# Layer-1 score and maximum matmuls over 128 zero-padded rows in a two-layer vision transformer

## The chip, the cores and the metric

The kernel runs on one core of a Trainium2 chip. The metric is device time in microseconds (us) of one execution, lower is better.

## What is computed

The input is 16 batches of 1024 tokens with 29 features. The reference embeds them, adds a position table and runs two transformer layers on each batch:

```python
h = tok(x, W)                                   # 1024 x 29 -> 1024 x 128, plus position table
h = h + attn0(layernorm(h))                     # group norm, 8 heads of 64, output projection, residual
h = h + ffn0(layernorm(h))                      # two lower-triangular 128 x 128 maps, gelu between
h = h + attn1(layernorm(h))                     # 8 heads of 16
h = h + switch_ffn(layernorm(h))                # 16 experts, one per token, capacity limit
# in both attentions, for every head of every batch:
scores = Q @ K.T * scale                        # 1024 x 1024
out = softmax(scores) @ V
```

The first layer (layer 0 below) has heads of 64 columns, the second (layer 1) heads of 16.

## The kernel before

Each head's softmax needs the row maxima before the exponentials. So the kernel computes all scores twice. The *maximum* pass (`max_tile`, TensorE at L766) makes 16 tiles of 128 queries by 512 keys for each head; VectorE reduces each to its row maximum (L1466). The maxima are transposed (L772), negated and copied to SBUF (L1022), and a DMA writes them as one more row of the query operand. The *score* pass (`scores`, TensorE at L790 and L792) makes tiles of 128 keys by 512 queries that already hold score minus maximum; ScalarE takes the exponential of each into `pr` (L1038).

For accuracy with matmuls in the fp32r format, every operand is split into a high and a low part, and the parts are stacked along the contraction rows. These operands are the *stacks*. In layer 0 a head's stacks fill 128 rows, with a second operand of 65 rows for the low terms and the maximum. In layer 1 a head has 16 columns, so a stack is 3 x 16 = 48 rows of products and row 48 for the maximum (a row of ones on the key side, minus the maximum on the query side). Before the change, one tile `stacks1[128, 2, 1024]` holds two heads of layer 1 at once: an even head in partitions 0 to 63, an odd head in partitions 64 to 127. The layer-1 maximum matmul contracts over 48 rows and its score matmul over 49. The stacks are filled by SP's DMA queue (`stack1` calls `move` with five copies; the fifth writes the row of ones), and `row` writes the maxima.

The exponentials times the values are `values0` (L808 for the high half, L809 for the low half, bf16, 129 columns each; the low half `pr_lo` is made at L461 by VectorE or GpSimd) and `values1` (L821, layer 1, four matmuls side by side on 32 output columns each, then `fold1` at L830). `outputs0` on VectorE (L1495, L1496) adds the high and low value sums of layer 0 into `on`, `normalize0` on GpSimd (L1183) scales them in place, and `heads_turn` on TensorE transposes 128 columns of `on` (two heads, a *chunk* c) for the output projection.

All engines follow one order written out in tables. A *unit* is 512 queries of one head, eight *steps* of 128 keys. There are five kinds of segment: "first" (layer 0 of batch 0, 16 units), "second" (layer 0 of batch 1 with layer 1 of batch 0, 32 units), "loop" (13 turns of 32 units; it also routes and runs the experts of the batch before, L752 and L1456), "penult" (as loop) and "final" (layer 1 of the last batch, 16 units). In the three kinds with both layers the units alternate: a layer-0 unit, then a layer-1 unit. Beside the score matmuls of a unit run the maximum tiles that `tile_step` gives (in a layer-1 unit, tiles of layer 1: in one layer-1 unit of two those of the same head, in the other those of the next head) and, at four of the eight steps (`VALUE_STEPS`), a fourth of the values of the unit before: sixteen L808 and L809 matmuls in a layer-1 unit, L821 and L830 in a layer-0 unit. After the units of a segment comes a serial part (`serial`): projections, norms, the feed-forward part.

A step of TensorE's order is:

```python
for step, at, layer, u, kt in steps_of(seg.kind):
    scores(seg, at, layer, u, kt)
    for tile in due_tiles(seg.kind, step):
        max_tile(seg, "now", *tile)
    if at > 0 and kt in VALUE_STEPS:
        values(seg, at - 1, VALUE_STEPS.index(kt))
```

The score pass and the maximum pass have two PSUM banks each, so TensorE waits when ScalarE has not taken the exponential two tiles back, or VectorE not the maximum two tiles back. VectorE works through one list in order: low parts, maxima, outputs, then experts.

Of the kernel before, what the change touches and what calls it, by code (L numbers as in the profile page):

```python
# [8 lines left out]
F32 = mybir.dt.float32  # L9
F32R = mybir.dt.float32r  # L10
# [5 lines left out]
P = 128  # L16
# [10 lines left out]
def units_of(kind):  # L27

    if kind == "first":
        return [(0, u) for u in range(16)]  # L30
    if kind == "final":
        return [(1, u) for u in range(16)]
    return [(layer, u) for u in range(16) for layer in range(2)]
# [245 lines left out]
def build(nc, x, tok_w, gn_w, gn_b, wq, bq, wk, bk, wv, bv, wo, bo, w1, b1, w2, b2,  # L279
          wq1, wk1, wv1, bq1, bk1, bv1, wo1, bo1, sw, sb_, ew, eb, pe, tri, out):  # L280
    NB, HH, WW, FT = x.shape
    S = HH * WW
    T = S // P
    C = tok_w.shape[1]
    H0, D0 = 8, 64
    H1, D1 = wq1.shape[0], wq1.shape[2]
    E = sw.shape[0]
    CAP = float(int(1.2 * (NB * S) / E))
    INNER = H0 * D0
# [4 lines left out]
    with ExitStack() as ctx:  # L294
        def sb(name, shape, dt=F32):
            return ctx.enter_context(nc.sbuf_tensor(name, shape, dt))

        def sem(name):
            return ctx.enter_context(nc.semaphore(name))
# [5 lines left out]
        ones = sb("ones", [P, P])  # L305
# [45 lines left out]
        k_lo, k_hi, q_hi, q_lo = (parts[:, n, :] for n in range(4))  # L351
        stacks = sb("stacks", [P, 2, 4, S], F32R)
        kB, kA, qA, qB = (stacks[:, :, n, :] for n in range(4))
        stacks1 = sb("stacks1", [P, 2, S], F32R)
        pr = sb("pr", [P, 2, T, HALF])
        pr_lo = sb("pr_lo", [P, T, HALF], BF16)
        mxh = sb("mxh", [P, 2, T, 2])
# [2 lines left out]
        o_hi = sb("o_hi", [P, 2, 2, D0])  # L360
        o_r = sb("o_r", [P, 4, 2])
        o_r1 = sb("o_r1", [P, 2, 4])
        on = sb("on", [P, T, INNER])
        on1 = sb("on1", [P, T, P])
        lg = sb("lg", [P, T, E])
        ex = sb("ex", [P, T, E])
# [18 lines left out]
        prep_pe = sem("prep_pe")  # L385
        prep_dve = sem("prep_dve")
        prep_pool = sem("prep_pool")
        x_loaded = Counts(sem("x_loaded"), 16)
        out_stored = Counts(sem("out_stored"), 16)
        hm_copied = Counts(sem("hm_copied"), 1)  # L390
# [39 lines left out]
        def await_drained(eng, seg, *names):  # L430
            plan = PLANS[seg.kind][0]
            for b in range(2):
                uses = [plan[name][1] for name in names if plan[name][0] == b]
                if uses:
                    eng.wait_ge(glue_drained[b].sem, glue_drained[b].at(seg, max(uses) + 1))
# [30 lines left out]
                    yield 8 * at + kt, at, layer, u, kt  # L466

        def k_stack(layer, head):
            return kB[:, head % 2] if layer == 0 else stacks1[64 * (head % 2):64 * (head % 2) + 64, 0, :]

        def q_stack(layer, head):
            return qB[:, head % 2] if layer == 0 else stacks1[64 * (head % 2):64 * (head % 2) + 64, 1, :]

        def max_row(layer):
            return 64 if layer == 0 else 3 * D1
# [4 lines left out]
        def await_stack(eng, b, layer, head):  # L480
            signal = stack_in(layer, head)
            eng.wait_ge(signal.sem, signal.at(b, 16 * (3, 5)[layer] * (head // 2 + 1)))

        @block.sync
        def _(sp):
# [23 lines left out]
                    sp.dma_start(dst, src).then_inc(load_small, 16)  # L509
            slot_free = sp.alloc_register("slot_free")  # L510
            sp.wait_ge(prep_dve, PREP_DVE)

            def load_x(b):
                sp.dma_start(xin[:, :, :], x_v[b.index()]).then_inc(x_loaded.sem, 16)

            def move(layer, head, moves):
                for dst, src in moves:
                    sp.dma_start(dst.bitcast(F32), src.bitcast(F32)).then_inc(stack_in(layer, head).sem, 16)
# [8 lines left out]
            def stack1(head, src):  # L527
                a, b_ = D1 * head, D1 * head + D1
                kk, qq = k_stack(1, head), q_stack(1, head)
                move(1, head, [(kk[0:2 * D1], src[a:b_, 0:2, :]),  # L530
                               (qq[0:2 * D1], src[a:b_, 2:3, :].broadcast_to([D1, 2, S])),
                               (kk[2 * D1:3 * D1], src[a:b_, 1, :]), (qq[2 * D1:3 * D1], src[a:b_, 3, :]),
                               (kk[3 * D1:3 * D1 + 1].rearrange("a (t q) -> a t q", t=T), ones[0:T, :])])

            def row(seg, name, layer, head, g):
                n = 2 * layer + g
# [66 lines left out]
        def _(te):  # L603
# [19 lines left out]
            def use(seg, name, *after):  # L623

                plan = PLANS[seg.kind][0]
                b, k = plan[name]
                needs = {b: k}
                for bank, count in (plan[other] for other in after):
                    needs[bank] = max(needs.get(bank, 0), count + 1)
                for bank, count in needs.items():  # L630
                    te.wait_ge(glue_drained[bank].sem, glue_drained[bank].at(seg, count))
                return glue[b], glue_filled[b].sem

            def turn(seg, name, src, rows_=P):
                bank, filled = use(seg, name)
                for j in range(4):
                    last = te.transpose(bank[0:rows_, j * P:(j + 1) * P], src(j), ident)
                last.then_inc(filled, 1)
# [45 lines left out]

            def heads_turn(seg, c, g):
                te.wait_ge(on_ready.sem, on_ready.at(seg.l0, 8 * (c + 1)))
                turn(seg, f"oT0.{c}.{g}", lambda j: on[:, 4 * g + j, c * P:(c + 1) * P])

            def done_heads(seg):
                AT = turn_slots(seg.kind)  # L690
# [64 lines left out]
            def max_tile(seg, when, layer, head, n):  # L755
                b = seg.layer(layer) if when == "now" else seg.following(layer)
                k = TILE_PLACES[seg.kind][when, layer, head, n]
                t, g = n // 2, n % 2
                if n == 0:
                    await_stack(te, b, layer, head)  # L760
                te.wait_ge(max_reduced.sem, max_reduced.at(seg, k - 1))
                if layer == 0:
                    qs, ks = qA[:, head % 2], kA[:, head % 2]
                else:
                    qs, ks = q_stack(1, head)[0:3 * D1], k_stack(1, head)[0:3 * D1]
                mm(maxb[k % 2][:, :], qs[:, t * P:(t + 1) * P], ks[:, g * HALF:(g + 1) * HALF],  # L766
                   start=True, stop=True).then_inc(max_filled.sem, 1)

# [13 lines left out]
            def scores(seg, at, layer, u, kt):  # L782
                b, k, head, g = seg.layer(layer), 8 * at + kt, u // 2, u % 2
                if kt == 0:
                    arrived = mrow_in[2 * layer + g]
                    te.wait_ge(arrived.sem, arrived.at(b, 16 * (head + 1)))
                te.wait_ge(exp_done.sem, exp_done.at(seg, k - 1))
                bank, q, kk = score[k % 2], slice(g * HALF, (g + 1) * HALF), slice(kt * P, (kt + 1) * P)
                if layer == 0:
                    mm(bank[:, :], kA[:, head % 2, kk], qA[:, head % 2, q], start=True, stop=False)  # L790
                last = max_row(layer) + 1
                mm(bank[:, :], k_stack(layer, head)[0:last, kk], q_stack(layer, head)[0:last, q],  # L792
                   start=(layer == 1), stop=True).then_inc(score_filled.sem, 1)

# [344 lines left out]
        def _(pool):  # L1139
# [38 lines left out]
            def normalize0(seg, at, jj):  # L1178
                _, u = units_of(seg.kind)[at]
                head, n, t = u // 2, 2 * u + jj, 4 * (u % 2) + 2 * jj  # L1180
                pool.wait_ge(o_drained.sem, o_drained.at(seg, o_place(seg.kind, 0, u, jj) + 1))
                o = on[:, t:t + 2, head * D0:(head + 1) * D0]
                pool.tensor_tensor(o, o, o_r[:, n % 4, :].unsqueeze(2).broadcast_to([P, 2, D0]), ALU.mult)\  # L1183
                    .then_inc(on_ready.sem, 1)

# [72 lines left out]
        def _(dve):  # L1258
            dve.memset(ones[:, :], 1.0).then_inc(prep_dve, 1)
            dve.memset(kB[64:65, :, :].bitcast(F32), 1.0)  # L1260
            dve.memset(v0[:, :, :, 2 * D0:2 * D0 + 2], 1.0)
            dve.memset(v1[:, :, :], 0.0).then_inc(prep_dve, 1)
            dve.memset(seen[:, :], 0.0)
# [4 lines left out]
            for n in range(2):  # L1268
                last = dve.tensor_tensor(pr[:, 1, 0, n * P:(n + 1) * P], pr[:, 0, 0, n * P:(n + 1) * P], lower, ALU.mult)
            last.then_inc(prep_dve, 1)  # L1270
            dve.wait_ge(prep_dve, 3)
            for c in range(NCH):
                last = dve.tensor_scalar(pr[:, 1, 1, c * P:(c + 1) * P], ones[:, :], bv_c[:, c:c + 1], None, ALU.mult)
# [213 lines left out]
            def outputs0(seg, at, jj):  # L1487
                _, u = units_of(seg.kind)[at]
                n, own = o_place(seg.kind, 0, u, jj), 2 * u + jj
                head, t = u // 2, 4 * (u % 2) + 2 * jj  # L1490
                dve.wait_ge(o_hi_out.sem, o_hi_out.at(seg, n + 1))
                bank = obank[n % 2][:, :].rearrange("p (j n) -> p j n", j=2)
                if own >= 4:
                    dve.wait_ge(on_ready.sem, on_ready.at(seg.l0, own - 3))
                dve.reciprocal(o_r[:, own % 4, :], bank[:, :, 2 * D0])  # L1495
                dve.tensor_tensor(on[:, t:t + 2, head * D0:(head + 1) * D0], bank[:, :, D0:2 * D0],  # L1496
                                  o_hi[:, own % 2, :, 0:D0], ALU.add).then_inc(o_drained.sem, 1)

            def outputs1(seg, at):
# [165 lines left out]
```

## Time and profile before

| | |
|---|---|
| three runs | median 9110.86 us (9104.55 to 9149.21) |
| profiled execution, its own time | 9088.71 us |
| its span, first to last instruction | 9086.9 us |
| TensorE busy in the span | 7605.5 us (84%) |
| VectorE / ScalarE / GpSimd busy | 57% / 36% / 18% |
| mean granted TensorE clock | 0.791 of full speed |

The profile is one execution. A busy TensorE is not necessarily one at its peak: matmuls are pipelined, and the granted clock has two levels, 1.0 (2.4 GHz) and 0.5 (1.2 GHz). A stretch with clock c spent 2 x (1 - c) of its time at the lower level. Durations of single matmuls overlap with their neighbours', so the cost of one is read from the distance between starts.

### The profile page before, as it was taken

How to read it: one execution, taken by the hardware profiler on the slowest of the kernel's cores; microseconds unless marked ns; L12 is line 12 of the kernel's file. 1: busy time of each engine (PE TensorE's matmuls, PEld its weight loads, DVE VectorE, ACT ScalarE, POOL GpSimd, SP SyncE). 2: the span in 40 equal slices, each digit the busy share in tenths (PEclk: the TensorE clock that was granted, in tenths of full speed). 3: DMA queues.
4: the chain of work that ended last, by engine and by line, in shares of the span. 5: the costliest groups of instructions: out<-in, count | busy, mean ns of one | idle time of the engine just before them, and what ended most of it. 6: DMA issues, size and time to landing. Idle time of an engine off the chain costs nothing.

```text
span 9086.9 us, 124508 instructions
## 1 busy us (share of the span) xinstructions
PE 7605.5 (84%) x39399; PEld 4583.5 (50%) x39399; DVE 5140.1 (57%) x11577; ACT 3263.9 (36%) x6291; POOL 1680.7 (18%) x1623
## 2 busy tenths in 40 slices
PE   6798888878888788887888878888787887879886
PEld 4565554445545455454554545555454554545542
DVE  5565656556555565655656555565565555655554
ACT  3343433334333343333433334333343333433331
POOL 2222211111111121111111111121111111111110
PEclk8887877878778787787877878777787777877877
DMA  2221101111021110211102111021111111101100
GB/s 58 51 44 28 36 21 46 36 31 36 21 46 35 31 40 16 54 27 37 36 14 54 27 39 36 12 54 27 39 36 23 44 27 39 36 22 43 27 23 9
DMA packets 89196, 309.01 MB, mean 34 GB/s; under 512 B 23942, under 2 KB 30022, under 8 KB 78278
## 3 DMA queue, kind: packets, MB, share of 16 engines
q1 hardware_dynamic: 88518, 300.53, 14.6%
q8 instruction: 357, 5.85, 0.3%
q14 instruction: 321, 2.63, 0.1%
HBM read 49.33 MB, written 41.94 MB: 10 GB/s over the span
## 4 chain that ended last, share of the span: by engine, by line
issue 67%; POOL 14%; PE 13%; DVE 4%; DMA 1%; POOLq 0%; SPq 0%; ACT 0%; DVEq 0%; ACTq 0%
POOL pr_lo L461 9%; PE bank L792 2%; POOL on L1183 2%; PE bank L766 2%; POOL on L1191 2%; PE bank L808 1%; PE bank L752 1%; PE bank L809 1%; PE bank L821 1%; PE bank L790 1%; DVE hm L1456 1%; DVE mxh L1466 1%; DMA stacks<-parts 1%; POOL rs L1158 1%; DVE pr_lo L461 0%
## 5 line engine op out<-in xcount | busy, mean ns | idle before, releaser
L1466 DVE TENSOR_REDUCE mxh<-bank 128x1 f32<-128x512 f32 x4096 | 2770.7, 688 | 2843.3 <-PE bank L766 2822.6
L1038 ACT ACTIVATE pr<-bank 128x512 f32<-128x512 f32 x4096 | 2410.2, 598 | 3065.4 <-PE bank L792 2984.8
L766 PE MATMUL bank<-stacks 128*128 128x512 f32 (+1 forms) x4096 | 2048.6, 509 | 860.9 <-DVE mxh L1466 824.8
L792 PE MATMUL bank<-stacks 65*128 65x512 f32 (+1 forms) x4096 | 2027.9, 502 | 11.8 <-ACT pr L1038 9.5
L766 PEld LDWEIGHTS bank<-stacks 128*128 128x128 f32 (+1 forms) x4096 | 910.4, 226 | 1265.3 <-DVE mxh L1466 1094.7
L808 PE MATMUL bank<-v,pr 128*128 128x129 bf16 x8192 | 1470.2, 269 | 3.3 <-DVE mT L461 2.4
L809 PE MATMUL bank<-v,pr_lo 128*128 128x129 bf16 x7936 | 1436.4, 270 | 0.0
L461 POOL TENSOR_TENSOR pr_lo<-pr 128x1024 bf16<-128x1024 f32 x496 | 938.8, 1893 | 2254.0 <-ACT pr L1038 2252.3
L792 PEld LDWEIGHTS bank<-stacks 65*128 65x128 f32 (+1 forms) x4096 | 875.0, 217 | 820.1 <-issue 573.6
L808 PEld LDWEIGHTS bank<-v,pr 128*128 128x128 bf16 x8192 | 988.5, 123 | 450.9 <-issue 444.6
L790 PE MATMUL bank<-stacks 128*128 128x512 f32 x2048 | 1111.0, 542 | 49.7 <-issue 41.7
L809 PEld LDWEIGHTS bank<-v,pr_lo 128*128 128x128 bf16 x7936 | 978.9, 123 | 0.0
L1183 POOL TENSOR_TENSOR on<-on,o_r 128x128 f32<-128x128 f32 x512 | 217.1, 424 | 3708.2 <-DVE on L1496 3708.2
L790 PEld LDWEIGHTS bank<-stacks 128*128 128x128 f32 x2048 | 424.4, 207 | 559.9 <-issue 423.8
L752 PE MATMUL bank<-ewT,mT 128*128 128x512 f32 x1024 | 652.6, 727 | 44.6 <-DVE hm L1456 44.6
L821 PE MATMUL bank<-pr,v 128*32 128x512 f32 x4096 | 650.7, 766 | 12.0 <-ACT pr L1038 12.0
L461 DVE TENSOR_TENSOR pr_lo<-pr 128x1024 bf16<-128x1024 f32 x496 | 603.5, 1217 | 40.1 <-ACT pr L1038 40.1
L1022 ACT ACTIVATE mrow<-bank 4x128 fp32r<-4x128 f32 x512 | 135.1, 264 | 1323.9 <-PE bank L772 1321.5
L1456 DVE SCALAR_TENSOR_TENSOR hm<-bank,wgt,hm 128x128 f32<-128x128 f32 x2048 | 552.4, 343 | 55.7 <-PE bank L752 48.6
L821 PEld LDWEIGHTS bank<-pr,v 128*32 128x32 f32 x4096 | 127.9, 130 | 360.5 <-issue 351.1
L1191 POOL TENSOR_TENSOR on<-on,o_r 128x64 f32<-128x64 f32 x256 | 192.1, 750 | 626.3 <-DVE on L1508 626.3
L973 ACT ACTIVATE parts<-bank,cols 128x512 fp32r<-128x512 f32 x256 | 176.2, 688 | 333.9 <-PE bank L648 330.2
(180 smaller groups left out, 5709.1 us busy)
## 6 DMA issues: line engine op xcount, KB each, us to landing
stacks<-parts SPq DMA_DIRECT2D x384, 512.0 KB, 6.7
parts_d<-pr SPq DMA_DIRECT2D x16, 2048.0 KB, 7.1
stacks<-parts_d SPq DMA_DIRECT2D x224, 128.0 KB
stacks<-parts_d SPq DMA_DIRECT2D x224, 64.0 KB
stacks<-mrow SPq DMA_DIRECT2D x512, 2.0 KB
out<-hm SPq DMA_DIRECT2D x16, 512.0 KB, 2.7
stacks<-pr SPq DMA_DIRECT2D x32, 128.0 KB
stacks<-pr SPq DMA_DIRECT2D x32, 64.0 KB
```

The lines of the kernel that those rows point to most:

```text
L461: return eng.tensor_tensor(low_of(seg.kind, u, kt - 1).rearrange("p a b -> p (a b)"), w, hi, ALU.subtract)
L752: mm(bank[:, :], mT[:, t * P:(t + 1) * P], ewT[:, 4 * q:4 * q + 4, :].rearrange("p e f -> p (e f)"), start=True, stop=True).then_inc(fille ...
L766: mm(maxb[k % 2][:, :], qs[:, t * P:(t + 1) * P], ks[:, g * HALF:(g + 1) * HALF], start=True, stop=True).then_inc(max_filled.sem, 1)
L790: mm(bank[:, :], kA[:, head % 2, kk], qA[:, head % 2, q], start=True, stop=False)
L792: mm(bank[:, :], k_stack(layer, head)[0:last, kk], q_stack(layer, head)[0:last, q], start=(layer == 1), stop=True).then_inc(score_filled.s ...
L808: mm(dst, hi, v0[:, kt, head, 0:w], start=(kt == 0), stop=False)
L809: last = mm(dst, lo, v0[:, kt, head, 0:w], start=False, stop=(kt == T - 1))
L821: last = mm(obank[n % 2][QUAD * r:QUAD * (r + 1), :], v1[:, kt, col:col + QUAD], pr[:, at % 2, kt, :], start=(kt < 4), stop=(kt >= 4))
L1038: act.activation(pr[:, at % 2, kt, :], score[k % 2][:, :], ACT.Exp, scale=SCALES[layer]).then_inc(exp_done.sem, 1)
L1183: pool.tensor_tensor(o, o, o_r[:, n % 4, :].unsqueeze(2).broadcast_to([P, 2, D0]), ALU.mult)\
L1456: ins = dve.scalar_tensor_tensor(hm[:, t, :], bank[:, e * P:(e + 1) * P], wgt[:, t, 4 * q + e:4 * q + e + 1], hm[:, t, :], ALU.mult, ALU.add)
L1466: dve.tensor_reduce(mxh[:, layer, n // 2, n % 2:n % 2 + 1], maxb[k % 2][:, :], AX_X, ALU.max)\
```

## The change

`stacks1` gets one tile of 128 rows for each of the two head buffers and each operand: `[128, 2, 2, 1024]`. It is filled with zeros once, in VectorE's prologue, and both head parities now lie in partitions 0 to 48. The layer-1 maximum and score matmuls contract over all 128 rows. The maximum matmul now also covers row 48, so the fifth copy of `stack1`, which wrote ones into the key side, instead writes a row of zeros (row 127 of the query side) over the old maxima of the query side; the ones are written once by two DMAs in SP's prologue, with a wait of their own (`ones_in`). `on` shrinks from four chunks of 128 columns to two that are used in turn, and `outputs0` waits at units 8 and 12 until the transposes of the chunk it overwrites have been drained.

```diff
-        stacks1 = sb("stacks1", [P, 2, S], F32R)
+        stacks1 = sb("stacks1", [P, 2, 2, S], F32R)
-        on = sb("on", [P, T, INNER])
+        on = sb("on", [P, T, 2 * P])
+        ones_in = sem("ones_in")
         def k_stack(layer, head):
-            return kB[:, head % 2] if layer == 0 else stacks1[64 * (head % 2):64 * (head % 2) + 64, 0, :]
+            return kB[:, head % 2] if layer == 0 else stacks1[:, head % 2, 0, :]
         def q_stack(layer, head):
-            return qB[:, head % 2] if layer == 0 else stacks1[64 * (head % 2):64 * (head % 2) + 64, 1, :]
+            return qB[:, head % 2] if layer == 0 else stacks1[:, head % 2, 1, :]
             sp.wait_ge(prep_dve, PREP_DVE)
+            for n in range(2):
+                sp.dma_start(stacks1[3 * D1:3 * D1 + 1, n, 0, :].rearrange("a (t q) -> a t q", t=T).bitcast(F32), ones[0:T, :])\
+                    .then_inc(ones_in, 16)
+            sp.wait_ge(ones_in, 32)
                                (kk[2 * D1:3 * D1], src[a:b_, 1, :]), (qq[2 * D1:3 * D1], src[a:b_, 3, :]),
-                               (kk[3 * D1:3 * D1 + 1].rearrange("a (t q) -> a t q", t=T), ones[0:T, :])])
+                               (qq[3 * D1:3 * D1 + 1], qq[P - 1:P])])
-                turn(seg, f"oT0.{c}.{g}", lambda j: on[:, 4 * g + j, c * P:(c + 1) * P])
+                turn(seg, f"oT0.{c}.{g}", lambda j: on[:, 4 * g + j, c % 2 * P:(c % 2 + 1) * P])
-                    qs, ks = q_stack(1, head)[0:3 * D1], k_stack(1, head)[0:3 * D1]
+                    qs, ks = q_stack(1, head), k_stack(1, head)
-                last = max_row(layer) + 1
+                last = max_row(0) + 1 if layer == 0 else P
-                o = on[:, t:t + 2, head * D0:(head + 1) * D0]
+                o = on[:, t:t + 2, head % 4 * D0:(head % 4 + 1) * D0]
             dve.memset(kB[64:65, :, :].bitcast(F32), 1.0)
+            dve.memset(stacks1[:, :, :, :].bitcast(F32), 0.0)
+                if u in (8, 12) and jj == 0:
+
+                    await_drained(dve, seg, f"oT0.{u // 4 - 2}.0", f"oT0.{u // 4 - 2}.1")
-                dve.tensor_tensor(on[:, t:t + 2, head * D0:(head + 1) * D0], bank[:, :, D0:2 * D0],
+                dve.tensor_tensor(on[:, t:t + 2, head % 4 * D0:(head % 4 + 1) * D0], bank[:, :, D0:2 * D0],
```

## Rows read from the trace of the kernel before

**Rows 1.** The page: TensorE's share of the span, and its clock in 40 slices (tenths).
```profile
PE 7605.5 (84%) x39399; PEld 4583.5 (50%) x39399; DVE 5140.1 (57%) x11577; ACT 3263.9 (36%) x6291; POOL 1680.7 (18%) x1623
...
PEclk8887877878778787787877878777787777877877
```

**Rows 2.** Groups by shape: count | busy us, mean ns of one | idle before.
```profile
L792 PE MATMUL bank<-stacks 49*128 49x512 f32 x2048 | 1147.8, 574 | 11.8 <-ACT pr L1038 9.5 <-DMA stacks<-mrow 0.2
L766 PE MATMUL bank<-stacks 48*128 48x512 f32 x2048 | 1127.3, 563 | 537.0 <-DVE mxh L1466 527.0 <-DMA stacks<-ones 5.1
...
L792 PE MATMUL bank<-stacks 65*128 65x512 f32 x2048 | 880.1, 430 | 0.0
```

**Rows 3.** Attention of whole segments (loop turns 1 and 5, second, final): stretch, length, busy, PEclk.
```profile
861.30:1344.70 483.40, 428.13 (x2251) 261.77 (x2249) 271.71 (x590) 181.93 (x356) 88.06 (x87) 0.78 0.12 27
...
3137.00:3604.30 467.30, 411.13 (x2251) 252.44 (x2249) 270.68 (x588) 181.50 (x356) 88.04 (x87) 0.81 0.12 28
...
8741.70:8963.30 221.60, 190.37 (x736) 76.63 (x734) 127.82 (x343) 83.19 (x162) 7.50 (x24) 0.75 0.05 15
...
402.40:773.30 370.90, 353.82 (x2135) 227.37 (x2133) 222.56 (x410) 177.51 (x352) 91.06 (x78) 0.82 0.15 33
```

**Rows 4.** Layer-0 units of loop turn 6: one unit, and the sum over its 16.
```profile
3858.90:3873.00 14.10, 12.14 (x53) 6.19 (x51) 8.87 (x20) 5.34 (x12) 4.18 (x3) 0.88 0.11 30
...
sum 200.80, PE 179.88 PEld 104.52 DVE 133.46 ACT 88.87 POOL 66.48; mean PE 11.24 PEld 6.53 DVE 8.34 ACT 5.55 POOL 4.16
```

**Rows 5.** Layer-1 units of the same turn: two of the 16, and their sum.
```profile
3821.70:3834.90 13.20, 12.81 (x96) 7.75 (x95) 9.10 (x17) 7.40 (x16) 1.97 (x3) 1.00 0.01 1
...
3873.00:3895.60 22.60, 19.01 (x88) 11.60 (x88) 9.50 (x23) 5.55 (x11) 0.69 (x2) 0.62 0.00 0
...
sum 267.20, PE 232.82 PEld 148.66 DVE 137.24 ACT 92.61 POOL 21.60; mean PE 14.55 PEld 9.29 DVE 8.58 ACT 5.79 POOL 1.35
```

**Rows 6.** A stretch inside the second of these units.
```profile
3881.00:3894.60 13.60, 13.60 (x62) 8.14 (x61) 2.94 (x6) 2.82 (x6) 0.40 (x1) 0.50 0.00 0
```

**Rows 7.** Timeline where that unit begins: start, length, engine, line [idle before].
```profile
3874.38 2.16 DVE L1456 SCALAR_TENSOR_TENSOR hm<-bank,wgt,hm 128x128 f32<-128x128 f32 x8
...
3876.45 1.22 DVE L461 TENSOR_TENSOR pr_lo<-pr 128x1024 bf16<-128x1024 f32 x1
...
3878.32 0.79 PE L766 MATMUL bank<-stacks 48*128 48x512 f32 x1 [3.59 <-DVE mxh L1466]
```

**Rows 8.** TensorE's timeline in a layer-1 unit, same head in both passes, clock 1.0.
```profile
3831.24 0.22 PE L809 MATMUL bank<-v,pr_lo 128*128 128x129 bf16 x1
3831.39 0.50 PE L792 MATMUL bank<-stacks 49*128 49x512 f32 x1
3831.73 0.39 PE L766 MATMUL bank<-stacks 48*128 48x512 f32 x1
3832.05 0.23 PE L808 MATMUL bank<-v,pr 128*128 128x129 bf16 x1
```

**Rows 9.** The same in the first segment, where all operands have over 64 rows.
```profile
102.59 0.40 PE L792 MATMUL bank<-stacks 65*128 65x512 f32 x1
102.83 0.40 PE L766 MATMUL bank<-stacks 128*128 128x512 f32 x1
103.07 0.23 PE L808 MATMUL bank<-v,pr 128*128 128x129 bf16 x1
```

**Rows 10.** TensorE's timeline in a layer-1 unit whose maximum tiles are the next head's.
```profile
3802.65 0.49 PE L792 MATMUL bank<-stacks 49*128 49x512 f32 x1
3802.65 0.49 PE L766 MATMUL bank<-stacks 48*128 48x512 f32 x1
3802.98 0.39 PE L792 MATMUL bank<-stacks 49*128 49x512 f32 x1
3802.99 0.39 PE L766 MATMUL bank<-stacks 48*128 48x512 f32 x1
```

**Rows 11.** Timeline of the prologue: VectorE's fill of v1 and its next wait.
```profile
3.70 1.06 DVE L1262 MEMSET v<- 128x1208 f32 x1 [0.20 <-issue]
...
20.61 0.37 DVE L1267 TENSOR_REDUCE fold<-tri_sb 128x32 f32<-128x128 f32 x1 [15.61 <-DMA pr<-in_L_ffn_switch_b]
```

**Rows 12.** The page, DMA issues: KB each, us from issue to landing.
```profile
xin<-in_x SPq DMA_DIRECT2D x16, 116.0 KB, 2.0
```

## The prediction

> **What bounds the kernel now.** I read the page first. TensorE is busy for 84% of the span, VectorE for 57%, and TensorE's clock stands at seven or eight tenths in nearly every slice, never at ten [rows 1]. So the busiest engine also runs slowly for a good part of the time.
>
> The second view is the groups by shape. A layer-1 score matmul (49 rows) takes 574 ns on average, a layer-0 one with the same 512 columns 430 ns [rows 2]. Where the clock is 1.0, both take 0.40 to 0.50 us [rows 8, 9]. So what differs is not the price of a row, but the clock under which each kind happens to run.
>
> The third view asks what the clock is worth. Two loop turns do the same work, 2251 matmuls each: one takes 483.4 us at 0.78, the other 467.3 us at 0.81 [rows 3]. The first spent 0.44 x 483.4 = 213 us at the lower level, the second 0.38 x 467.3 = 178 us. So 35 us more at the lower level cost 16.1 us: 0.46 us for each. It would be 0.5 if TensorE alone set the time. I use 0.45 (all turns that I compared lie near it). The kernel is bound by TensorE, and by TensorE's clock.
>
> The fourth view says where the low time lies. I cut one loop turn into its 32 units. Adding 2 x (1 - clock) x length over them, the 16 layer-0 units spent 43 us of 200.8 us at the lower level [rows 4], the 16 layer-1 units 138 us of 267.2 us [rows 5]. The reader is to compare two neighbours. The layer-0 unit at 3858.9 has the clock 0.88 over 14.1 us, so 3.4 us low: it falls and is back at once [rows 4]. The layer-1 unit behind it has 0.62 over 22.6 us, so 17.2 us low [rows 5]. It begins with 3.59 us in which TensorE waits: VectorE works through eight expert updates (2.16 us) and a low part (1.22 us) before it takes the next maximum [rows 7]. The clock falls there and then doesn't come back, though TensorE is busy without a gap: for 13.60 of 13.60 us at 0.50 [rows 6]. What sets it apart from a layer-0 unit is the rows: of a layer-1 unit's columns about half (sixteen matmuls of 512 against 64 of 129) pass over 48 or 49 rows. A layer-1 unit can also keep the full clock (3821.7, 1.00, 13.2 us [rows 5]); it has a head's projections with 128 rows in it.
>
> So the trace speaks for a clock that follows how many rows of the array work, not only for how long it is busy. The Trainium skill, "TensorE: Matmul & The Clock Gate", Part 1, says that the clock is set by how busy TensorE has been recently and rises after sustained activity; the stretch of 13.60 us fully busy at 0.50 doesn't agree with that if busy means any matmul.
>
> **The change part by part.**
>
> *Layer-1 matmuls over 128 rows, effect on the clock.* Nothing about a matmul's own columns changes. The layer-1 stretches get the shapes of the layer-0 stretches. The falls themselves stay, since their cause is VectorE's list. What should change is the recovery. In a loop turn 13 of the 16 layer-1 units have low time, 3.4 us at the least and 17.4 us at the most, 138 us in all; two of them stand in [rows 5]. If each of the 13 recovers as the layer-0 unit does, in 3.4 us, 44 us are left. If each needs twice that, 88 us. If the padding also stops the falls, 0. I take 50 us, near the first, because that is the nearest row. The saving is 88 us low, times 0.45 = 40 us a turn. The 13 turns and "penult" make 14: 554 us. Bounds: 14 x 0.45 x 50 = 315 us and 14 x 0.45 x 138 = 870 us.
>
> "Second" takes 370.9 us at 0.82, so 133 us low, and "final" 221.6 us at 0.75, so 111 us low [rows 3]. "Second" has no experts, and "final" only a few beside layer 1. I take 80 us off each, times 0.45 = 36 us each, 72 us. Bounds 40 and 100 us. The serial parts and "first" have none of these matmuls and keep their time.
>
> *Effect on the order of matmuls, same head.* In half of the layer-1 units both passes work on one head. With values around them the distances between starts at full clock are 0.15 (L809 to L792), 0.34 (L792 to L766) and 0.32 us (L766 to L808): 0.81 us [rows 8]. Where all operands exceed 64 rows, the second and third are 0.24 and 0.24 us [rows 9], and from one value matmul to the next it is 0.06 us, the nearest row for the first. That is 0.54, or 0.27 us less, at four steps a unit. There are 15 segments with 8 such units: 120 x 4 x 0.27 = 130 us. The Trainium skill, "TensorEngine Tiling (Array Packing)", Key Properties, says that changing the tiling mode drains TensorE; the extra 0.08 to 0.10 us on both sides of the value matmuls is what such a drain would show as, and by it these gaps go.
>
> *Next head.* In the other half the score matmul and the maximum matmul lie in different halves of the partitions, and they start at the same 0.01 us: pairs every 0.33 us, both for the price of one [rows 10]. Padded, they need 0.24 each. At the four steps with values the old chain is 0.15 + 0 + 0.42 = 0.57 us (the 0.42 is the pair's 0.33 and the extra 0.09) against 0.54; at the four others 0.33 against 0.48. That is 4 x 0.15 less 4 x 0.03 = 0.48 us worse: 120 x 0.48 = 58 us lost. At the lower level all of these distances about double. The Trainium skill, "TensorE: Matmul & The Clock Gate", in its closing table, speaks against this change: small-K matmuls in distinct row groups run concurrently, and K = 32 alone takes as long as K = 128; the trace agrees with the pairs, and padding gives this up.
>
> Both together: 130 - 58 = 72 us, times 0.9 for what lies on the path (0.45 of 0.5): 65 us. Bounds: 130 us gained, if the lost pairs are hidden behind ScalarE; and if the extra gaps stay, nothing is gained and eight pairs a unit cost 0.24 us each, 120 x 8 x 0.24 x 0.9 = 207 us lost.
>
> *Zeros and ones.* VectorE fills 4096 columns; 1208 took 1.06 us, so 3.6 us, ahead of a wait of 15.61 us for loads [rows 11]: nothing, and 3.6 us without that cover. SP issues two small DMAs and waits for them before the first `load_x`. The nearest row is 2.0 us to landing [rows 12], plus two issues: 3 us, once, on the path, between 0 and 5. Behind that wait stand SP's first load and all of the embedding.
>
> *The fifth copy of `stack1`.* A row of 4 KB from one partition replaces eight pieces of 512 B, at the same place in SP's queue. TensorE waited 5.1 us in all on the old one [rows 2], so the effect is between a gain of 5 us and a few us lost: nothing. The stacks are due 24 steps before their first tile, so a faster TensorE doesn't overtake them.
>
> *`on` in two chunks.* Units 8 and 12 wait for the drain of transposes that were issued at steps 78 and 142, while the outputs come at steps 140 and 204 (in "first" at 44 and 76 against 76 and 108). With 32 steps and more between them the wait has been met when it is reached, so it costs nothing. Were it not, VectorE's maxima would queue behind it, and TensorE behind these.
>
> *Sum.* 554 + 72 + 65 - 3 = 688 us less. From the profiled execution's 9088.7 us (span 9086.9) that is 8401 us. The median shown lies 0.24% higher, so 8420 us. I say 8410.
>
> **The rivals.**
>
> *A: likeliest.* As summed. With all bounds at one end it is 9111 - 870 - 100 - 130 = 8011 us, with all at the other 9111 - 315 - 40 + 207 + 5 = 8968 us. They won't all fall on one side; its own range is 8150 to 8700 us. Chance 0.68.
>
> *B: the clock rises, VectorE takes the time.* At full clock TensorE's idle gaps behind VectorE weigh more, each can bring a new fall, and layer-1 units with experts stay near 18 us instead of 22.6. For it: L766 already waited 527 us for VectorE [rows 2], and the stall of 3.59 us has nothing to do with TensorE [rows 7]. Against it: a unit with 9.10 us of VectorE's work was done in 13.2 us at full clock [rows 5]. About half of the gain remains: 8750 us (8700 to 8900). Chance 0.13.
>
> *C: the clock doesn't follow the padded rows.* The clock may look only at busy time, or rows of zeros may not count as work. No matmul of this trace multiplies stacks of zeros, so no row excludes it. Against the first, the 13.60 us at 0.50 [rows 6]. Then the order's 65 us remain, and 3 us are lost: 9050 us, between 8980 and 9110. By the Trainium skill's rule of the busy TensorE ("TensorE: Matmul & The Clock Gate", Part 1) this case, with its 9050 us, is the one to expect. Chance 0.12.
>
> *D: slower.* C, and the drains stay as well, so that only the lost pairs are left. 120 units x 8 pairs make 960. Each costs 0.24 us at full clock and twice that, 0.48, at the lower level, 0.36 in the middle: 346 us, times 0.9 = 311 us, so 9422 us. It decides as soon as the clock in layer-1 units stays under about 0.80 and the gaps of [rows 8] don't shrink; the pairs of [rows 10] speak for it. Chance 0.07.
>
> **How the numbers follow.** 0.5% of 9111 us is 46 us, about what a measurement of this kernel can tell from no change. A and B are faster. C is faster by over 46 us in 0.07 and within it in 0.05. D is slower. That makes 0.88, 0.05 and 0.07. A and B hold 0.81, so the range is theirs: 8150 to 8900.
>
> **What would show it.** The mean clock of the span rises from 0.79 to about 0.86; that of layer-1 units to near 0.88, with no stretch of over 10 us at 0.50 in them. L766 and L792 of layer 1 come to 430 to 470 ns mean, all start apart, and the distances of [rows 8] become those of [rows 9]. Serial parts keep their length. If the clock stays at 0.79, C or D is right, and the distances tell which. If it rises and units with experts don't shrink below 18 us, it is B. The forecast is wrong in size if the falls themselves vanish (faster than 8150) or recovery takes longer than a layer-0 unit's.

## The result, and the profile after

The changed kernel takes 8245.07 us in the median (8236.99 to 8252.57, 4 runs) against 9107.70 us of the kernel before (9100.57 to 9149.21, 4 runs). The ratio is 0.9044, with a 95% interval of 0.9015 to 0.9074. The profiled execution took 8252.57 us, its span is 8250.8 us, its mean granted clock 0.861. The forecast of 8410 us (8150 to 8900) lies on the right side, and the time lies inside its range; the gain is 863 us where 700 were forecast.

The page, TensorE's and the clock's lines, answer to [rows 1]:

```profile
PE 6712.0 (81%) x39399; PEld 4321.9 (52%) x39399; DVE 5134.2 (62%) x11578; ACT 3222.9 (39%) x6291; POOL 1681.3 (20%) x1623
...
PEclk8898888889888898888988889888898888989887
```

The number of matmuls is the same. No slice of the clock is below 8 but the last. The groups by shape (count | busy us, mean ns of one | idle before) answer to [rows 2]:

```profile
L771 PE MATMUL bank<-stacks 128*128 128x512 f32 x4096 | 1858.3, 456 | 937.5 <-DVE mxh L1472 900.0 <-DMA stacks<-parts 23.4 <-DMA stacks<-stacks 5.1
...
L797 PE MATMUL bank<-stacks 128*128 128x512 f32 x2048 | 1095.1, 537 | 8.0 <-ACT pr L1043 7.9
...
L797 PE MATMUL bank<-stacks 65*128 65x512 f32 x2048 | 862.1, 421 | 0.0
```

The new fifth copy (`stacks<-stacks`) holds TensorE up for 5.1 us in all, as the old one did.

The attention of a loop turn, of "second" and of "final" (stretch, length, busy times, PEclk), answer to [rows 3]:

```profile
1321.00:1741.20 420.20, 360.00 (x2251) 238.26 (x2249) 271.08 (x588) 178.81 (x357) 88.09 (x87) 0.89 0.14 31
404.40:718.80 314.40, 293.94 (x2135) 202.61 (x2133) 222.02 (x410) 175.06 (x352) 91.10 (x78) 0.97 0.18 39
7925.60:8126.20 200.60, 168.52 (x736) 88.58 (x735) 127.08 (x343) 84.13 (x162) 7.48 (x23) 0.88 0.06 17
```

A turn's attention took 467.3 and 483.4 us in [rows 3]; the one shown here takes 420.2 us. "Second" went from 370.9 to 314.4 us, "final" from 221.6 to 200.6 us. The same turn as in [rows 4] and [rows 5] cut into its units: first a layer-0 unit and the sum over the 16 of layer 0, then two layer-1 units and the sum over their 16.

```profile
4022.30:4036.40 14.10, 11.95 (x53) 6.71 (x52) 9.05 (x20) 5.26 (x12) 4.19 (x3) 0.88 0.10 30
...
sum 201.30, PE 179.17 PEld 106.41 DVE 136.09 ACT 88.74 POOL 65.56; mean PE 11.20 PEld 6.65 DVE 8.51 ACT 5.55 POOL 4.10
```

```profile
3987.90:3999.60 11.70, 10.72 (x96) 7.94 (x95) 8.97 (x17) 6.99 (x14) 2.04 (x3) 1.00 0.01 2
...
4036.40:4052.70 16.30, 12.62 (x87) 9.09 (x86) 9.33 (x23) 5.21 (x11) 0.69 (x2) 0.79 0.00 0
...
sum 218.60, PE 180.65 PEld 131.84 DVE 134.84 ACT 90.07 POOL 22.54; mean PE 11.29 PEld 8.24 DVE 8.43 ACT 5.63 POOL 1.41
```

All of this turn's gain lies in the layer-1 units: 267.2 us became 218.6 us. The unit of 22.6 us at 0.62 [rows 5] takes 16.3 us at 0.79, 6.8 us of it low instead of 17.2. Added up over the 16 units, 50 us are low instead of 138. Also look at the first of the two. It had the full clock before as well, and still went from 13.2 to 11.7 us. So the clock isn't all.

### The profile page after: what moved, and what is told of

The parts are those of the page before. It is cut to its first block, busy times and chain, and to the rows that moved or that the text cites. A ratio compares the mean times of both kernels' runs of the same rounds, so it can differ in the third digit from the quotient of the medians.

```text
span 8250.8 us, 124569 instructions
## 1 busy us (share of the span) xinstructions
PE 6712.0 (81%) x39399; PEld 4321.9 (52%) x39399; DVE 5134.2 (62%) x11578; ACT 3222.9 (39%) x6291; POOL 1681.3 (20%) x1623
## 4 chain that ended last, share of the span: by engine, by line
issue 65%; POOL 16%; PE 12%; DVE 4%; DMA 1%; POOLq 1%; SPq 0%; ACT 0%; DVEq 0%; ACTq 0%
POOL pr_lo L462 9%; PE bank L771 2%; POOL on L1188 2%; POOL on L1196 2%; PE bank L797 2%; PE bank L757 1%; DVE mxh L1472 1%; PE bank L813 1%; DVE hm L1462 1%; PE bank L814 1%; PE bank L826 1%; PE bank L795 1%; DMA stacks<-parts 1%; POOL rs L1163 1%; DVE pr_lo L462 1%
## 5 line engine op out<-in xcount | busy, mean ns | idle before, releaser
L771 PE MATMUL bank<-stacks 128*128 128x512 f32 x4096 | 1858.3, 456 | 937.5 <-DVE mxh L1472 900.0
L797 PE MATMUL bank<-stacks 65*128 65x512 f32 (+1 forms) x4096 | 1957.3, 479 | 8.0 <-ACT pr L1043 7.9
L771 PEld LDWEIGHTS bank<-stacks 128*128 128x128 f32 x4096 | 850.5, 208 | 1452.3 <-DVE mxh L1472 1193.2
L813 PE MATMUL bank<-v,pr 128*128 128x129 bf16 x8192 | 1229.5, 242 | 3.3 <-DVE mT L462 2.4
L814 PE MATMUL bank<-v,pr_lo 128*128 128x129 bf16 x7936 | 1176.0, 240 | 0.0
L795 PE MATMUL bank<-stacks 128*128 128x512 f32 x2048 | 1073.9, 524 | 47.2 <-issue 40.9
L813 PEld LDWEIGHTS bank<-v,pr 128*128 128x128 bf16 x8192 | 871.6, 109 | 296.1 <-issue 277.3
L797 PEld LDWEIGHTS bank<-stacks 65*128 65x128 f32 (+1 forms) x4096 | 837.8, 205 | 320.1 <-issue 178.1
L814 PEld LDWEIGHTS bank<-v,pr_lo 128*128 128x128 bf16 x7936 | 865.6, 109 | 0.0
L795 PEld LDWEIGHTS bank<-stacks 128*128 128x128 f32 x2048 | 410.9, 201 | 508.7 <-issue 347.9
L826 PE MATMUL bank<-pr,v 128*32 128x512 f32 x4096 | 617.4, 730 | 12.0 <-ACT pr L1043 12.0
L757 PE MATMUL bank<-ewT,mT 128*128 128x512 f32 x1024 | 568.7, 641 | 42.9 <-DVE hm L1462 42.9
```

Of the source, the lines that this page charges most:

```text
L757: mm(bank[:, :], mT[:, t * P:(t + 1) * P], ewT[:, 4 * q:4 * q + 4, :].rearrange("p e f -> p (e f)"), start=True, stop=True).then_inc(fille ...
L813: mm(dst, hi, v0[:, kt, head, 0:w], start=(kt == 0), stop=False)
L814: last = mm(dst, lo, v0[:, kt, head, 0:w], start=False, stop=(kt == T - 1))
L826: last = mm(obank[n % 2][QUAD * r:QUAD * (r + 1), :], v1[:, kt, col:col + QUAD], pr[:, at % 2, kt, :], start=(kt < 4), stop=(kt >= 4))
```

## The experiments

Two theories stood against each other at first. **R**: the clock follows the rows of the array in use. **M**: what counts is to stay in shapes of over 64 rows; the gaps at each alternation go, and the clock rises because of that. Each pad size is an edit of two lines of the changed kernel; N is 48 and 49, 64, 65 or 96:

```diff
-                    qs, ks = q_stack(1, head), k_stack(1, head)
+                    qs, ks = q_stack(1, head)[0:N], k_stack(1, head)[0:N]
-                last = max_row(0) + 1 if layer == 0 else P
+                last = max_row(0) + 1 if layer == 0 else N
```

**48 and 49 rows.**

> The changed kernel, but the layer-1 matmuls contract over 48 and 49 rows of the padded tiles again, both heads in partitions 0 to 48. No pairs can form. Theory R (the clock follows the rows of the array in use): the mean clock falls back to 0.77 to 0.80 and the time lies above the kernel before, 9150 to 9450 us, since the pairs are gone and the extra gaps beside the value matmuls stay. Theory B (the gain came from something other than rows, such as one tile per head, the ones written once or the two chunks): the time stays near 8250 us.

Measured: 9516.3 us, ratio 1.045 (1.0378 to 1.0523), span 9512.1 us, clock 0.761. Its page:

```profile
PEclk8877777777777777777777777777787777877766
```

The clock lies just below R's range and the time above it, on R's side and far from B's. The whole gain hangs on the rows; of ones written once, one tile per head and two chunks no gain is left to see. The kernel is 425 us of span slower than the one before, since the pairs are gone as well. But most of that is the clock again: 4547 us are low instead of 3798, which at 0.45 makes 337 us, and 88 us are left for the pairs as such.

**65 rows.**

> The changed kernel with 65 rows in both layer-1 matmuls. More than 64 rows, so the extra gaps of 0.08 to 0.15 us beside the value matmuls should be gone as with 128 rows, but little over half of the rows are in use. Theory R: the clock is between, 0.80 to 0.84, and the time 8600 to 8950 us. Theory M (what counts is to stay in the mode of over 64 rows, and the clock rose only because the gaps went): clock 0.86 and 8250 to 8300 us.

Measured: 8605.84 us, ratio 0.945 (0.9374 to 0.9527), span 8588.5 us, clock 0.821. R, at the lower end of the time. M as it stands falls: in shapes of over 64 rows throughout, the clock is still far from 0.861.

**96 rows.**

> The changed kernel with 96 rows. Theory R: most of the gain, clock 0.84 to 0.86, 8280 to 8500 us, between 65 and 128 rows. Theory M: the same as 65 and 128 rows, 8250 to 8300 us.

Measured: 8363.55 us, ratio 0.9184 (0.9117 to 0.9252), span 8370.1 us, clock 0.846. With 65, 96 and 128 rows the clock is 0.821, 0.846 and 0.861 and the span 8588.5, 8370.1 and 8250.8 us: more rows of zeros, a faster kernel. In low time (2 x (1 - clock) x span) these are 3075, 2578 and 2294 us. So 781 us less of it saved 338 us, 0.43 us each; the forecast used 0.45. None of these three kernels crosses 64 rows in layer 1, and their columns are the same, so this line shows the effect of the rows by itself.

**Halves of 64 rows.** The kernel before, with each half of its one tile padded to 64 rows. The pairs of [rows 10] stay possible. The ones are again written once by two DMAs in SP's prologue; those lines are left out here:

```diff
+            dve.memset(stacks1[:, :, :].bitcast(F32), 0.0)
-                               (kk[3 * D1:3 * D1 + 1].rearrange("a (t q) -> a t q", t=T), ones[0:T, :])])
+                               (qq[3 * D1:3 * D1 + 1], qq[63:64])])
-                    qs, ks = q_stack(1, head)[0:3 * D1], k_stack(1, head)[0:3 * D1]
+                    qs, ks = q_stack(1, head), k_stack(1, head)
-                last = max_row(layer) + 1
+                last = max_row(0) + 1 if layer == 0 else 64
```

> The kernel before with its two heads in the halves of one tile, but each padded with zeros to 64 rows, so that the matmuls use 64 rows and the next head's maxima can still run at the same time as the scores. Theory R: a little of the clock comes back (48 and 49 rows become 64), mean 0.80 to 0.83 and 8750 to 9050 us. Theory M: nothing changes against before, 9080 to 9130 us, since the gaps stay.

Measured: 8857.43 us, ratio 0.9727 (0.9653 to 0.98), span 8866.9 us, clock 0.811. R again: here the shapes alternate exactly as often as before (2794 changes between at most 64 rows and over 64 in both traces), and the clock still rises.

**64 rows, the next size below 65.**

> The changed kernel with 64 rows in both layer-1 matmuls, against the run with 65: one row less, but the shapes alternate again between at most 64 and over 64 rows, 2726 times in the program. Theory G (each of these alternations costs a gap of about 0.1 us beside the clock): 200 to 320 us above the 65-row run, 8800 to 8930 us, with the clock down by no more than 0.01 or 0.02. Rival (gaps are hidden, all of the difference is low time): within 60 us of the 65-row run. Against the kernel with halves of 64 rows, which has the pairs: 100 to 300 us slower if the pairs are worth what the run with 49 rows suggests.

Measured: 9083.85 us, ratio 0.9986 (0.9969 to 1.0004), span 9110.6 us, clock 0.802. One row less costs 478 us, more than theory G said, and the rival's 60 us is excluded. (The two ran on different chips; by their ratios to the kernel before, 0.9986 and 0.945, it comes out the same.) Its low time is 3608 us, 533 more than with 65 rows, which at 0.45 explains 240 us of the 522 us between the spans. The other 282 us go to the alternations. The traces have 2794 changes between at most 64 rows and over 64 with 64 rows, and 100 with 65; the expectation's 2726 also counts changes to matmuls of at most 32 rows. So it is 0.10 us for each of 2694. A layer-1 unit at full clock in both shows them without the clock. First with 64 rows, then with 65:

```profile
4409.40:4422.60 13.20, 12.79 (x95) 7.77 (x95) 9.07 (x17) 7.42 (x16) 2.04 (x3) 1.00 0.00 1
```

```profile
4155.30:4167.10 11.80, 10.83 (x96) 8.02 (x95) 8.98 (x17) 7.08 (x15) 2.09 (x3) 1.00 0.01 2
```

The same unit at the same clock takes 1.4 us less. The waits of TensorE's weight loads for "issue" (in total, times, longest), again 64 rows and then 65:

```profile
PEld bank L797 <- issue: 614.4, 1276, 1.7
PEld bank L813 <- issue: 477.3, 1013, 0.7
```

```profile
PEld bank L813 <- issue: 313.8, 947, 0.5
PEld bank L797 <- issue: 186.6, 679, 1.7
```

The gap can also be read without any price for the clock. I took each entry into a group of layer-1 matmuls together with the exit behind it, wherever both traces have the same clock and TensorE isn't idle, and compared the distances between the same starts. With 64 rows an entry and its exit take 0.31 us more at clock 1.0 (463 places) and 0.36 us more at 0.5 (204 places). For the 1347 entries that would be some 410 to 490 us of TensorE's own time (an estimate); 282 us of it reached the time of the kernel.

The Trainium skill, "TensorEngine Tiling (Array Packing)", Key Properties, says that a change of the tiling mode drains TensorE. These runs agree that such a change costs time: the step from 64 to 65 rows removes about 0.10 us of the kernel's time an alternation.

Against the halves of 64 rows the run is 244 us longer in span, with 256 us more low time (115 us). About 129 us are left for the pairs that the halves can run at once.

**The two chunks of `on` alone**, on the kernel before.

> The kernel before with only the two chunks of on and the wait at units 8 and 12. Both theories: no change, 9050 to 9150 us (ratio 0.998 to 1.002), since the transposes waited for were drained 32 steps and more earlier.

Measured: 9151.6 us against 9122.65 us, ratio 1.0024 (1.0005 to 1.0042). No gain; if anything it costs 0.2%, at the edge of what was expected (ratio up to 1.002).

**The changed kernel again, and nonzero rows.** The second kernel fills the pad rows of the key side with 0.7:

```diff
-            dve.memset(stacks1[:, :, :, :].bitcast(F32), 0.0)
+            dve.memset(stacks1[:, :, 0, :].bitcast(F32), 0.7)
+            dve.memset(stacks1[:, :, 1, :].bitcast(F32), 0.0)
```

> The changed kernel once more, on the same chip as the next two, 8230 to 8260 us, to compare them with it.

> The changed kernel with the key side's pad rows filled with 0.7 instead of zeros; the query side's pad rows stay zero, so the products don't change. Theory R: rows count as rows whatever is in them, ratio to the changed kernel 0.998 to 1.002. Theory Z (zeros count for less): the clock rises further, by 0.005 or more, and the time falls below 8220 us.

Measured: 8243.59 us (ratio to before 0.9029, 0.9005 to 0.9053) and 8248.29 us (0.9033, 0.9009 to 0.9058), clocks 0.863 and 0.862. Rows of zeros on the key side count like any. With both sides nonzero nothing was tried, since the sums would change.

**Layer 0 padded too.** Its second score operand has 65 rows. Rows 64 to 127 of `kB` and `qB` are filled with zeros once, and the matmul uses 128 (the line that makes `zeroed` is left out):

```diff
+            for n in range(2):
+                dve.memset(kB[64:128, n, :].bitcast(F32), 0.0)
+                dve.memset(qB[64:128, n, :].bitcast(F32), 0.0).then_inc(zeroed, 1)
+            dve.wait_ge(zeroed, 2)
             dve.memset(kB[64:65, :, :].bitcast(F32), 1.0)
-                last = max_row(0) + 1 if layer == 0 else P
+                last = P
```

> The changed kernel, and also the second operand of the layer-0 score matmul padded from 65 to 128 rows with zeros. Theory R: the layer-0 units lose some of their low time too (their clock is 0.90 on average, 40 us low of 201 us a turn), mean clock 0.87 to 0.88, 8130 to 8220 us. Theory M (only the mode of over 64 rows counts): no change, since 65 rows are already in that mode.

Measured: 8129.98 us, ratio to before 0.8906 (0.8883 to 0.893), clock 0.877. That is 114 us below the changed kernel on the same chip. Here no shape newly crosses 64 rows, and no column is added. M expected no change, R forecast it.

**Short updates.** What is left of the low time? The start of the unit at 4036.4 answers to [rows 7]:

```profile
4037.85 2.16 DVE L1462 SCALAR_TENSOR_TENSOR hm<-bank,wgt,hm 128x128 f32<-128x128 f32 x8
...
4039.93 1.22 DVE L462 TENSOR_TENSOR pr_lo<-pr 128x1024 bf16<-128x1024 f32 x1
...
4041.80 0.79 PE L771 MATMUL bank<-stacks 128*128 128x512 f32 x1 [3.68 <-DVE mxh L1472]
```

The wait is as long as before, and the L771 behind it takes 0.79 us again.

```diff
-dve.scalar_tensor_tensor(hm[:, t, :], bank[:, e * P:(e + 1) * P], wgt[...], hm[:, t, :], ...)
+dve.scalar_tensor_tensor(hm[:, t, 0:8], bank[:, e * P:e * P + 8], wgt[...], hm[:, t, 0:8], ...)
```

> The changed kernel with the expert updates of VectorE cut from 128 to 8 columns (the other 120 columns of the expert sum are left out), so that the eight updates take about 0.6 us instead of 2.16. Theory S (what is left of the low time in layer-1 units begins in VectorE's list, when TensorE waits for the maxima): the low time of the units with experts falls, mean clock 0.87 to 0.90, 7900 to 8100 us. Rival (the falls have another cause): only the stall itself shrinks, the clock stays at 0.86 to 0.865, 8100 to 8180 us.

Measured: 7726.19 us, ratio 0.85 (0.8424 to 0.8576), span 7753.2 us, clock 0.894. The kernel leaves out 120 of the 128 columns of the expert sum, so it only measures. Theory S holds; the time is below its range of 7900 to 8100 us, though eight short updates still took 1.16 us, not 0.6. The unit of 16.3 us at 0.79 becomes

```profile
3841.50:3854.40 12.90, 10.20 (x87) 7.11 (x86) 8.32 (x23) 5.07 (x11) 0.69 (x2) 1.00 0.00 0
```

Low time fell by 650 us, 293 us at 0.45; the other 205 us of 498 are within the 256 us that 256 groups of updates, each 1.00 us shorter, can shorten the stalls by.

**Experts' matmuls moved in even units**, on the kernel with both layers padded:

```diff
-        first = [8 * m + 5 for m in (7, 11, 12, 13, 14, 15, 19, 20, 21, 22, 23, 24, 26, 27, 28, 29)]
+        first = [8 * m + (5 if m % 2 else 2) for m in (7, 11, 12, 13, 14, 15, 19, 20, 21, 22, 23, 24, 26, 27, 28, 29)]
```

> The kernel with both layers padded once more, 8120 to 8165 us, to compare the next one with it on one chip.

> Both layers padded, and the experts' matmuls of even units moved from step 5 to step 2 of the unit, so that VectorE's eight updates no longer stand directly before the last low part at the start of a layer-1 unit. Theory S: the wait of 3.6 us at the start of layer-1 units with experts shrinks to under 2 us and falls less often, clock 0.88 to 0.90, 7950 to 8100 us. Rival: the wait only moves into the layer-0 unit, where the updates meet the low part and the outputs of step 4, and the time stays within 30 us of the kernel with both layers padded.

Measured: 8143.86 us (ratio 0.8937, 0.8907 to 0.8967) and 7820.7 us (0.8576, 0.8546 to 0.8605), clocks 0.878 and 0.906. The same layer-1 unit, unmoved and then moved, with the sum over 16 such units of the turn:

```profile
3974.90:3991.30 16.40, 12.71 (x88) 9.19 (x87) 9.38 (x23) 5.24 (x11) 0.69 (x2) 0.79 0.00 0
...
sum 218.70, PE 181.07 PEld 132.20 DVE 134.48 ACT 89.95 POOL 22.10; mean PE 11.32 PEld 8.26 DVE 8.40 ACT 5.62 POOL 1.38
```

```profile
3846.40:3858.10 11.70, 10.21 (x87) 7.05 (x86) 7.34 (x16) 4.71 (x10) 1.60 (x2) 1.00 0.00 0
...
sum 190.80, PE 167.87 PEld 120.69 DVE 120.71 ACT 86.57 POOL 28.38; mean PE 10.49 PEld 7.54 DVE 7.54 ACT 5.41 POOL 1.77
```

The unit of 22.6 us in the kernel before is down to 11.7 us at full clock, with the updates still done in full. The wait at the start of the unit, 3.69 us unmoved, is 0.68 us here, with one of 1.49 us further on:

```profile
3846.03 0.50 PE L772 MATMUL bank<-stacks 128*128 128x512 f32 x1 [0.68 <-DVE mxh L1477]
...
3849.55 0.50 PE L772 MATMUL bank<-stacks 128*128 128x512 f32 x1 [1.49 <-DVE mxh L1477]
```

In the whole program TensorE's waits of over 3 us before a maximum matmul went from 105 to 8 by the move. The layer-0 unit ahead of it got longer, 15.20 us:

```profile
3831.20:3846.40 15.20, 12.29 (x54) 6.78 (x52) 10.79 (x28) 5.70 (x12) 4.19 (x3) 0.89 0.10 28
```

It takes the updates' 2.16 us, but stays at 0.89. Clock and time both lie past what theory S expected (0.88 to 0.90, 7950 to 8100 us), and the rival falls. This kernel is the fastest that computes all of the reference.

## Why the prediction was right, and where its size was off

*The clock term.* Right in mechanism: padding raised the clock, and the low stretches got shorter. Its size came out close in part by luck. The forecast left 50 us low in the layer-1 units of turn 6, and 50 us were measured. But it had all 13 falls stay and each recover nearly as fast as in a layer-0 unit, in 3.4 us. In fact 10 of the 16 units have low time, 5.0 us each on average, and up to 6.9 us where experts run. Fewer falls and a slower recovery cancel. In the whole program the traces have 433 low stretches of 8.8 us on average before and 361 of 6.4 us after. Turn 6 was also one of the turns with the least low time before: 195 us in its attention, where the 14 turns have 206 us on average. Over the span, low time fell from 2 x 0.209 x 9086.9 = 3798 us to 2 x 0.139 x 8250.8 = 2294 us. These 1504 us are worth 677 us at 0.45, where 554 + 72 = 626 us were forecast. "Second" gave more than its 36 us (56.5 us in all), because its clock went to 0.97; "final" gave 21 us, not 36, in part because 48 us of it stayed low, where 31 were allowed.

*The order term.* This is the step that was mis-sized, at 65 us. Of the 836 us between the spans, 159 us are left after the clock, and the forecast had 65. Its distances were nearly right. With 128 rows, same head and full clock, they are now 0.03, 0.31 and 0.24 us, 0.58 in all, against 0.81 in [rows 8] and a forecast of 0.54:

```profile
3996.50 0.22 PE L814 MATMUL bank<-v,pr_lo 128*128 128x129 bf16 x1
3996.53 0.48 PE L797 MATMUL bank<-stacks 128*128 128x512 f32 x1
3996.84 0.40 PE L771 MATMUL bank<-stacks 128*128 128x512 f32 x1
3997.08 0.23 PE L813 MATMUL bank<-v,pr 128*128 128x129 bf16 x1
```

What was wrong is the count. The prediction priced the gaps beside values only, at 4 steps of 240 units, so 960 entries and 960 exits at most, and half of these at almost nothing. But TensorE also enters and leaves the small shape around the experts' matmuls (284 entries from L752), transposes (304), projections (90) and at each change from a layer-0 unit (225, from L766). The trace of before has 2694 more changes between at most 64 rows and over 64 than that of after, half of them exits and half entries. At 0.10 us each that is 282 us, measured between 64 and 65 rows, where the forecast had a gain of 130. Against it stand the lost pairs, 129 us by the halves of 64 rows; the forecast had 58. The difference of 153 us is close to the 159 us left over. That is less of a proof than it seems, since these runs lie on the way from the one kernel to the other: it says that the two other steps, halves padded to 64 rows and 65 rows to 128, leave next to nothing beside their low time (19 and -13 us). The split between clock and order rests on 0.45 us for each us of low time, and the runs show 0.43 on the line of pad sizes; the remainder is uncertain by some 30 us.

*The zeros, the fifth copy, the chunks.* As forecast, nothing or nearly: attention starts at 86.6 us instead of 84.5 (3 were allowed, once), the fifth copy still costs 5.1 us in all, and the two chunks alone 0.2%.

*The signs.* The mean clock is 0.861, that of the layer-1 units in turn 6 is 0.89, and serial parts keep their length (68 us a turn). Low stretches of over 10 us within attention went from 120 to 15, all at the start of a segment's attention. One sign failed: L771 has 456 ns on average, within 430 to 470, but the layer-1 form of L797 has 537. It now starts 0.03 us behind a value matmul that is still running, so its recorded time holds a wait, and as a price it misleads.

*The rivals.* B would have left units with experts near 18 us; they are at 15.4 to 16.5. The wait for VectorE is still there (106 waits of over 3 us before a maximum matmul, before and after), but its price was mostly the slow clock behind it. C falls with the whole series of pad sizes: zeros count, and the busy share of TensorE went down (84% to 81%) while its clock went up. The Trainium skill's rule in "TensorE: Matmul & The Clock Gate", Part 1, is that activity releases the throttle. These runs don't agree with it if activity is busy time alone: with 48 and 49 rows TensorE ran at 0.761, with 128 rows and the same instructions at 0.861. D lost because the clock moved. Without pad and pairs the kernel does take 9516 us, and D had said 9422, but that nearness is chance: D had the lost pairs cost 311 us at an unchanged clock, and they cost 88 to 129 us, the rest being low time.

## What to carry to other kernels

If TensorE is the bound and its granted clock is below full, look at which shapes run in the low stretches: matmuls over few rows can keep it low even without a gap (0.50 for 13.60 us in [rows 6]). Padding the contraction with zeros to 128 rows costs no columns, and here was worth more than running two small matmuls at once. Then look for the wait that starts each fall; moving one engine's work by three steps was worth another 323 us here.

## What was not expected

One row, from 64 to 65, is worth 478 us. Splitting this shows two effects of like size: the alternation of shapes (0.10 us each, 282 us) and 533 us more at the lower level, worth 240 us. One row more can hardly be what raises the clock by that much: from 65 to 96 rows the low time fell by 497 us, 16 us a row. That the gaps also hold the clock down is likely, but it is only argued; no run takes the two apart. A whole-kernel effect of VectorE's expert updates was also larger than their time: cutting 256 groups of eight from 2.16 to 1.16 us saved 498 us of span, by this split 205 of them the stalls and 293 the clock.
